# Graph attention over 32 graphs on one core: another opening, from the weights' peaks to the first batch's heads

## What is computed

```python
h = jnp.maximum(_layernorm(x), 0.0)
q, k, v = heads(h @ Wq + bq), heads(h @ Wk + bk), heads(h @ Wv + bv)   # 6 heads of 64
scores = einsum('bhqd,bhkd->bhqk', q, k) / sqrt(64)
probs = softmax(scores + where(adj, 0.0, -9e15), axis=-1)
ctx = einsum('bhqk,bhkd->bhqd', probs, v).reshape(b, s, 384)
out = x + ctx @ Wf + bf
```

## Time and profile before

| | us |
|---|---|
| median of 3 runs | 677.98 |
| lowest and highest | 676.17, 678.21 |
| the profiled execution | 679.02 |
| its span, first to last instruction | 677.0 |

### The profile page before, as it was taken

How to read it: one execution, slowest core, us unless ns; L and a number is a source line. 1 busy time by engine, 2 the same in 40 slices (tenths; PEclk the granted TensorE clock), 3 DMA queues, 4 the chain that set the end, 5 groups by cost and what they waited for, 6 DMA issues and landing times. The chain is left out here.

```text
span 677.0 us, 20551 instructions
## 1 busy us (share of the span) xinstructions
PE 628.2 (93%) x6644; PEld 510.3 (75%) x6644; DVE 513.2 (76%) x1548; ACT 506.7 (75%) x1164; POOL 423.5 (63%) x459
## 2 busy tenths in 40 slices
PE   7638899999899998999999999999999999999985
PEld 5426788888788886888778877788878888888863
DVE  5626787788788877788778887788878888887774
ACT  1435888888788886788878876788778888888872
POOL 1335666767666666776666667576666776676551
PEclk8878899999999999999999999999999999999999
DMA  7015678767787686667877676776878668767563
GB/s 241 20 34 112 127 149 159 154 149 127 160 154 160 150 162 121 150 145 158 159 145 159 153 146 120 154 160 152 159 141 155 146 141 160 160 137 134 127 136 94
DMA packets 207684, 95.89 MB, mean 142 GB/s; under 512 B 152817, under 2 KB 207602, under 8 KB 207602
## 3 DMA queue, kind: packets, MB, share of 16 engines
q1 hardware_dynamic: 207602, 94.69, 67.7%
HBM read 17.05 MB, written 12.58 MB: 44 GB/s over the span
## 5 line engine op out<-in xcount | busy, mean ns | idle before, releaser
L632 DVE CUSTOM_DVE_ANT_0 logits<-scores,mask,logit_unscale 128x256 f32<-128x256 f32 x384 | 170.6, 481 | 128.0 <-PE scores L916 124.6
L432 POOL TENSOR_TENSOR p_rows<-probs,p_rows 128x512 f16<-128x512 f32 x128 | 151.0, 1180 | 183.1 <-ACT p_rows L513 183.1
L503 ACT ACTIVATE probs<-logits,raised 128x256 f32<-128x256 f32 x384 | 174.2, 500 | 6.3
L856 PE MATMUL ring<-h_hi,w_hi 128*128 128x256 f16 x576 | 159.1, 276 | 2.6 <-DVE w_lo L723 2.6
L857 PE MATMUL ring<-h_lo,w_hi 128*128 128x256 f16 x576 | 158.8, 276 | 0.0
L858 PE MATMUL ring<-h_hi,w_lo 128*128 128x256 f16 x576 | 158.6, 275 | 0.0
L416 POOL TENSOR_TENSOR split<-qk,split 128x512 f16<-128x512 f32 x96 | 111.1, 1157 | 13.1 <-DVE split L656 13.1
L915 PE MATMUL scores<-heads 128*128 128x256 f16 x384 | 95.3, 275 | 23.0 <-DMA heads<-split 16.9
L499 ACT ACTIVATE raised<-least,p_raise 128x2 f32<-128x2 f32 x192 | 56.8, 296 | 68.4 <-DVE least L632 53.3
L525 ACT ACTIVATE qk<-ring,qk_bias_s,qkv_ratio 128x256 f32<-128x256 f32 x192 | 97.0, 555 | 9.4 <-PE ring L858 8.6
L943 PE MATMUL ctx<-v_hi,p_cols 128*128 128x65 f16 x768 | 89.5, 194 | 14.0 <-DMA p_cols<-p_rows 9.8
(11 more groups left out here) (90 smaller groups left out, 1427.2 us busy)
## 6 DMA issues: line engine op xcount, KB each, us to landing
heads<-split SPq DMA_DIRECT2D x192, 96.0 KB, 2.2
x_in<-in_x_dram SPq DMA_DIRECT2D x32, 384.0 KB, 3.4
heads<-split SPq DMA_DIRECT2D x192, 64.0 KB, 2.1
out_dram<-result SPq DMA_DIRECT2D x64, 192.0 KB, 2.1
adj_in<-in_adj_dram SPq DMA_DIRECT2D x32, 64.0 KB, 2.0
p_cols<-p_rows SPq DMA_TRANSPOSE x128, 3.1
w_raw<-in_L_gnn_Wq_dram SPq DMA_DIRECT2D x1, 576.0 KB, 4.3
w_raw<-in_L_gnn_Wk_dram SPq DMA_DIRECT2D x1, 576.0 KB, 6.3
```

The costliest lines, as they stand in the source:

```text
L432: pool.tensor_tensor(p_rows[u][:, 1], probs[u % 3][:], p_rows[u][:, 0], ALU.subtract).then_inc(p_lo_ready, 1)
L503: act.activation(probs[u % 3][:, a], logits[u % 3][:, a], ACT.Exp, bias=raised[u % 3][:, a:a + 1], scale=-1.0).then_inc(probs_ready, 1)
L632: dve.tensor_tensor_reduce(out=logits[u % 3][:, a], in0=score_bank[u % 2][:, a * S:(a + 1) * S], in1=mask[b.parity][:, t], scale=logit_uns ...
L856: pe.matmul(out_ap, a_hi, m_hi, start=first, stop=False)
```

## The change

- The joining over partitions no longer uses `partition_all_reduce`. TensorE transposes the peak column, broadcast to 128 columns, into a bank (`spread_peaks`), and VectorE reduces it over its free axis (`join_peaks`).
- There are three joins instead of two: q's and k's peaks with their biases, then v's, then Wf's. Each is followed by `powers` for its own columns, so v's scale no longer comes with those of q and k.
- The factors (`qkv_ratio` for q and k, `logit_unscale`, `mask_scale`, `qk_bias_s`) are made on GpSimd by eight small operations, that of v on VectorE.
- The biases are loaded from ScalarE's queue, at its very start; ScalarE then runs one `Exp` ahead of everything.
- The cycle with b.k = -1 is gone. Its work is written out in the preambles of the engines in another order, with 14 more warm-up matmuls on TensorE between the spread of the peaks and the first projection.
- Batch 0's v is projected and split in cycle 0, behind the second unit; Wv's peak, scale and parts come behind those of q and k. Wf's peak, scale and parts move to other places of cycle 0.
- `bf_full` is copied by ScalarE instead of VectorE.
- SyncE issues `place_heads(0, 0)`, `place_heads(0, 1)` and the load of the third adjacency ahead of cycle 0.
- `project_qk(b, 1)` waits for `v_lo` of the batch before, where it had no such wait (batches 1 and 2).

```diff
+WARM_UPS_MORE = 14
...
-            for k in range(-1, FIRST_IN_LOOP):
+            for k in range(FIRST_IN_LOOP):
...
-            def load_column(dst, src):
-                sp.dma_start(dst, src.rearrange("(c p) -> p c", p=P),
-                             allow_slow_non_contiguous=True).then_inc(small_in, 16)
-            load_column(qk_bias[:, 0], bq)
-            load_column(qk_bias[:, 1], bk)
-            load_column(bv_col[:], bv)
-            sp.dma_start(bf_row[:], bf.rearrange("(a n) -> a n", a=1)).then_inc(small_in, 16)
+            place_heads(Batch(0, 0), 0)
+            place_heads(Batch(0, 0), 1)
+            sp.wait_ge(mask_ready, 2)
+            load_adj(Batch(0, 2))
...
-            pool.wait_ge(peak_ready, 6)
-            pool.partition_all_reduce(qkv_peak_all[:], qkv_peak[:], P, ALL_MAX).then_inc(peaks_joined, 1)
-            pool.wait_ge(factors_ready, 2)
+            def chained(count):
+                pool.wait_ge(pool_chain, count)
+            pool.wait_ge(small_in, 64)
+            pool.wait_ge(scales_ready, 1)
+            pool.tensor_tensor(qkv_ratio[:, 0:2], qkv_scale[:, 2:4], qkv_unscale[:, 0:2],
+                               ALU.mult).then_inc(pool_chain, 1)
+            pool.tensor_tensor(logit_product[:, 0:1], qkv_unscale[:, 2:3], qkv_unscale[:, 3:4],
+                               ALU.mult).then_inc(pool_chain, 1)
+            pool.tensor_tensor(logit_product[:, 1:2], qkv_scale[:, 2:3], qkv_scale[:, 3:4],
+                               ALU.mult).then_inc(pool_chain, 1)
+            for n in range(2):
+                pool.tensor_scalar(qk_bias_s[:, n], qk_bias[:, n], qkv_scale[:, 2 + n:3 + n], None,
+                                   ALU.mult).then_inc(factors_ready, 1)
+            chained(3)
+            pool.tensor_scalar(qkv_ratio[:, 0:2], qkv_ratio[:, 0:2], 1.0 / H_SCALE, None,
+                               ALU.mult).then_inc(factors_ready, 1)
+            pool.tensor_scalar(logit_unscale[:], logit_product[:, 0:1], -1.0 / D ** 0.5, None,
+                               ALU.mult).then_inc(factors_ready, 1)
+            pool.tensor_scalar(mask_scale[:], logit_product[:, 1:2], -NEG * D ** 0.5, None,
+                               ALU.mult).then_inc(factors_ready, 1)
+            pool.wait_ge(factors_ready, 5)
+            make_mask(Batch(0, 0))
+            split_lo(Batch(0, 0), 0)
+            normalise(Batch(0, 1))
+            split_lo(Batch(0, 0), 1)
+            split_lo(Batch(0, 0), 2)
+            pool.wait_ge(bf_ready, 1)
+            add_bias(Batch(0, 0))
...
-                    if first:
-                        pool.wait_ge(peak_ready, 7)
-                        pool.partition_all_reduce(f_peak_all[:], f_peak[:], P, ALL_MAX).then_inc(peaks_joined, 1)
-                        pool.wait_ge(bf_ready, 1)
...
+            def load_column(dst, src):
+                act.dma_start(dst, src.rearrange("(c p) -> p c", p=P),
+                              allow_slow_non_contiguous=True).then_inc(small_in, 16)
+            load_column(qk_bias[:, 0], bq)
+            load_column(qk_bias[:, 1], bk)
+            load_column(bv_col[:], bv)
+            act.dma_start(bf_row[:], bf.rearrange("(a n) -> a n", a=1)).then_inc(small_in, 16)
+            act.wait_ge(pool_const, 5)
+            act.activation(bv_wide[:, 0], zeros[:], ACT.Exp).then_inc(table_loaded, 1)
+            act.wait_ge(table_loaded, 1)
+            h_hi_part(Batch(0, 0))
+            act.wait_ge(scales_ready, 1)
+            for j in range(C):
+                for n in range(2):
+                    weights_hi(n, pair(j))
+            act.wait_ge(factors_ready, 5)
+            qk_full(Batch(0, 0), 0)
             act.wait_ge(small_in, 64)
...
             for c in range(C):
                 act.activation(bv_wide[:, c], zeros[:], ACT.Identity,
                                bias=bv_col[:, c:c + 1]).then_inc(wide_ready, 1)
+            qk_full(Batch(0, 0), 1)
+            qk_full(Batch(0, 0), 2)
+            act.wait_ge(bias_ps_ready, 1)
+            act.activation(bf_full[:], ctx_bank[:, 0:H], ACT.Copy).then_inc(bf_ready, 1)
+            act.wait_ge(scales_ready, 2)
+            weights_hi(2)
-                if front and not first:
+                if front:
+                    if b.k != 0:
+                        v_hi_part(b, 1)
+                    exps(b, 1)
+                if b.k == 0:
+                    v_hi_part(b, 0)
-                    exps(b, 1)
+                if here:
...
-                if b.k == 0:
-                    act.wait_ge(scales_ready, 2)
-                    weights_hi(3)
+                if b.k == 0:
+                    act.wait_ge(scales_ready, 3)
+                    weights_hi(3)
...
+            def join_peaks(spread, cols, nth):
+                dve.wait_ge(peaks_spread, nth)
+                n = cols.stop - cols.start
+                dve.tensor_reduce(peak_all[:, cols], spread[:, 0:n * P].rearrange("p (n q) -> p n q", n=n), AX_X,
+                                  ALU.max).then_inc(peaks_joined, 1)
+                dve.wait_ge(peaks_joined, nth)
...
+            join_peaks(pt_bank, slice(0, 4), 1)
...
+            powers(slice(0, 4), qkv_bound, qkv_scale, qkv_unscale, 1)
             h_lo_part(Batch(0, 0))
-            dve.wait_ge(peaks_joined, 1)
...
-            weights_lo(0, 1, pair(0))
-            weights_lo(1, 2, pair(0))
...
-            dve.wait_ge(factors_ready, 2)
+            for j in range(C):
+                for n in range(2):
+                    weights_lo(n, 2 * j + n + 1, pair(j))
+            qk_hi_part(Batch(0, 0), 0)
+            layer_stats(Batch(0, 1), (0, 1))
+            qk_hi_part(Batch(0, 0), 1)
+            weight_peak(2, peak[:, 4:5])
+            qk_hi_part(Batch(0, 0), 2)
+            join_peaks(pt_bank, slice(4, 5), 2)
+            step(dve.tensor_scalar(qkv_bound[:, 4:5], peak_all[:, 4:5], LEAST, None, ALU.max),
+                 dve.tensor_scalar(qkv_bound[:, 5:6], peak_all[:, 4:5], float(H), LEAST, ALU.mult, ALU.max))
+            powers(slice(4, 6), qkv_bound, qkv_scale, qkv_unscale, 2)
+            step(dve.scalar_tensor_tensor(out=qkv_ratio[:, 2:3], in0=qkv_scale[:, 5:6], scalar=1.0 / H_SCALE,
+                                          in1=qkv_unscale[:, 4:5], op0=ALU.mult, op1=ALU.mult))
+            weights_lo(2, 7)
-                dve.wait_ge(peaks_joined, 2)
+                join_peaks(ring[1], slice(5, 6), 3)
...
-                if front and not first:
+                if front:
-                if first:
-                    weights_lo(0, 3, pair(1))
-                    weights_lo(1, 4, pair(1))
-                    weights_lo(2, 5)
+                if b.k == 0:
+                    v_lo_part(b, 0)
+                if here:
                     v_lo_part(b, 1)
                 if (b + -2).exists():
                     finish(b + -2, 1)
-                if first:
-                    weights_lo(0, 6, pair(2))
-                    weights_lo(1, 7, pair(2))
-                    dve.wait_ge(bias_ps_ready, 1)
-                    dve.tensor_copy(bf_full[:], ctx_bank[:, 0:H]).then_inc(bf_ready, 1)
                 if b.k == 0:
-                    scale_output()
+                    weight_peak(3, peak[:, 5:6])
+                    layer_stats(b + 2, (0, 1))
...
-                if first:
-                    layer_stats(b + 2, (0, 1))
...
-                if first:
+                if b.k == 0:
+                    scale_output()
-                if b.k == 0:
-                    weights_lo(3, 8, pair(0))
-                    weights_lo(3, 8, pair(1))
...
-                    weights_lo(3, 8, pair(2))
+                    weights_lo(3, 8)
...
+                elif j == 1 and (b + -1).exists():
+                    wait(pe, v_lo_ready, (b + -1).count(2, 1))
-                        pe.wait_ge(w_lo_ready, 2 * j + n + (2 if j == C - 1 else 1))
+                        pe.wait_ge(w_lo_ready, 2 * j + n + 1)
...
-                    pe.wait_ge(w_lo_ready, 5)
+                    pe.wait_ge(w_lo_ready, 7)
...
+            def spread_peaks(bank, cols):
+                for n in range(cols.start, cols.stop):
+                    o = (n - cols.start) * P
+                    mm = pe.transpose(bank[:, o:o + P], peak[:, n:n + 1].to_broadcast([P, P]), ident[:])
+                mm.then_inc(peaks_spread, 1)
+            pe.wait_ge(peak_ready, 4)
+            spread_peaks(pt_bank, slice(0, 4))
+            for _ in range(WARM_UPS_MORE):
+                pe.matmul(ring[2][:, 0:P], zeros[:], zeros[:], start=True, stop=True)
+            for j in range(C):
+                project_qk(Batch(0, 0), j)
...
+            pe.wait_ge(peak_ready, 5)
+            pe.wait_ge(peaks_joined, 1)
+            spread_peaks(pt_bank, slice(4, 5))
...
-                if front and not first:
+                if front:
+                if b.k == 0:
+                    project_v(b, 0)
+                    project_v(b, 1)
...
+                if b.k == 0:
```

(42 more changed lines are left out.)

34 lines of the change are left out of this document (8 added, 26 removed).

## The result

| | before | after |
|---|---|---|
| time, median (range) of 4 runs each | 678.10 (676.17 to 680.93) us | 685.32 (685.06 to 686.99) us |
| span of the profiled execution | 677.0 us | 683.4 us |
| first `apply_probs(0, 3)`, the mark | 70.08 us | 55.48 us |
| batch that holds a jump back of the loop, mean of five | 20.96 us | 24.54 us |

The ratio is 1.0097, with a 95% interval from 1.0068 to 1.0126: slower by 1%, where 660.7 us was forecast. The opening did what was forecast (14.6 us earlier at the mark, 15.8 forecast); the loop, which nobody edited, gave it all back and 7 us more.

A forecast was written before the change was run, and what follows sets the result against it. TensorE's work was taken to bound the loop, a chain of waits the opening. An earlier mark (15.8 us) plus saved half clock (1.5) gave 17.3 off 679.02, 661.7; less 1.04 to the median, 660.7 us, range 655.8 to 667.0.

The forecast's parts named there:

- What bounds the kernel: Loop bound by TensorE's work (busy 98.7 us of 100), opening by a chain of waits; nothing in the loop edited.
- Loads: Opening: biases moved to ScalarE's queue cost Wk between 0 and 2.0 us, taken as 1.2.
- Joins: Opening, joining the peaks: four transposes 0.65 us, one reduction 0.6 to 0.7, done at 12.1, scale at 13.3.
- Weights and projections: Opening: weight parts start at 13.3 us, first projection at 14.9 at full clock, projections end at 20.8.
- Factors: Opening: eight tiny operations on GpSimd, 0 to 6 us in all, taken as 1.5 and hidden by the weights.
- Batch 0: Opening: scores of units 0 and 1 at 23.9 and 28.1 us, `split_lo(1, 0)` at 44.2 against 56.05.
- The mark: First `apply_probs(0, 3)` at 54.3 us against 70.08, gain 15.8; with 1.5 of half clock saved, 17.3.
- The sum: Whole run: 679.02 us less 17.3 is 661.7; less 1.04 from profiled execution to median, 660.7.
- (a) to (c): Three rivals; the middle one: GpSimd stays the bound, gain 11.9 us, 666.1; chance 0.17, dear factors included.
- (a): Rival, opening: no clock falls on TensorE and biases come free; gain 20.3 us, time 657.7; chance 0.21.
- (c): Rival, opening: GpSimd's standstills are not due to `partition_all_reduce`, 13.9 us come back; gain 3.4, 674.6; chance 0.04.
- (d): Rival, loop: TensorE waits each cycle on GpSimd's chain, clock falls, 1.5 us each; slower, up to 705.7; chance 0.02.

The follow-up runs named there:

- e3: The kernel after with its hardware loop written out, so no jump back: 657.64 us, ratio 0.9668 to before.
- e4: The kernel before with its hardware loop written out, so no jump back: 673.72 us, ratio 0.9900 to before.
- e1: The kernel after with 44 empty TensorE instructions ahead of its first cycle, moving the loop's head: 654.51 us, ratio 0.9621 to before.
- e5: The kernel before with 112 empty TensorE instructions in cycle 0, loop head at 1482 as in e1: 670.02 us, ratio 0.9854 to before.
- e8: The kernel before, loop written out as in e4, with only Wf's peak joined by TensorE and VectorE instead of GpSimd: 663.62 us, ratio 0.9745.
- e14: The kernel after with 145 empty TensorE instructions ahead of its cycles; single execution, only the loop read: 21.15 us for a batch with a jump.
- e13: The kernel after with 256 empty TensorE instructions ahead of its cycles; single execution, only the loop read: 24.27 us for a batch with a jump.
- e12: The kernel after with 44 empty instructions where TensorE waits, and v's join, scale and split moved behind unit 0: 652.35 us, ratio 0.9585.

## Why the prediction was wrong, step by step

- *What bounds the kernel.* Right for the opening. Wrong in one sentence, "Nothing in the loop is edited", from which I took "the loop's period unchanged": the sum has no term for the jumps back. The 1.3 us of idle in the earlier trace rows were read as a rounding of a full TensorE. 0.91 of them were the standstill of one jump (340.48), and the word "issue" beside `scores` at 184.21, 261.59 and so on stood in the trace of before. I had read that word as a cause on GpSimd and never asked for it on TensorE.
- *Loads.* 1.2 taken; Wk is 0.58 later (8.05 to 8.63), nearer to the lower end.
- *Joins.* Four transpositions 0.65 as forecast, the reduction 0.69 (0.6 to 0.7), done at 11.54 (12.1).
- *Weights and projections.* `w_hi` at 12.67 (13.3), first projection at 14.36 (14.9) at full clock, as forecast.
- *Factors.* 1.5 taken, 2.55 measured: eight operations of 0.19 to 0.56 us. They end at 15.34, and `qk_full` began at 16.59: hidden.
- *Batch 0.* Scores of units 0 and 1 at 23.54 and 27.48 (23.9, 28.1). `mask_and_max(0, 0)` at 28.49 (27.8): of v's tiny steps, three took 0.51, 0.92 and 0.71 beside GpSimd's `split_lo` and `add_bias`, where the first two had taken 0.17 in the first join. The larger miss is the clock. I gave TensorE half clock for some 3.5 us behind its gap; it had it from 29.2 to 36.0, 6.8 us. So the 18 matmuls of v, taken as 2.9 us at full clock, ran from 31.31 to 36.56, 5.2 us, and `v_lo(0, 1)` ended at 38.0 (35.4). `layer_stats(2)` then ends at 40.8 (38.3), `split_lo(1, 0)` at 46.5 (44.2). Ahead of `apply_probs(0, 1)` I gave half clock once more; that did not come, the clock is 1.00 from 36 to 70.

```profile
30.00:35.00 5.00, 4.60 (x16) 2.57 (x17) 1.13 (x5) 2.52 (x6) 0.00 (x0) 0.50 0.30 86
...
36.00:70.00 34.00, 27.69 (x287) 22.29 (x286) 25.83 (x80) 25.09 (x57) 23.25 (x25) 1.00 0.51 102
```

- *The mark.* 55.48 (54.3). With no jumps the opening is worth 16.1 us (e3, e4); with jumps that cost nothing 15.8 (e1, e5), or about 13.8 without the empty instructions; against 17.3. So this term was 1.2 to 3.5 too large. The mark itself is 1.2 late, with `layer_stats(2)` 2.5 late ahead of it; what each part of the delay costs at the mark no run took apart.
- *The sum* left out a term, and this is the step that made a gain into a loss: five jumps at 24.54 - 20.96 = 3.6 us, 17.9. With it and the tail (34.5 us behind the last `add_bias`, 33.0 before) the spans come out: 677.0 - 13.6 + 18.5 + 1.5 = 683.4.
- *The rivals.* (a) to (c) did not happen; (a)'s full clock is refuted by the half clock from 29.2 to 36.0, (c) by e8. (d) had the mechanism, a repeated wait of TensorE with a fall of the clock, and came at 0.02 because I put it on GpSimd's chain and gave "the loop's code is untouched" as the reason against it. The code was untouched; its place was not. The price that I gave, 1.5 us a time from 12 times on, was of no use either: it was 3.6, at five places.

## What to carry to other kernels

An edit ahead of a hardware loop moves the loop in the instruction stream, and that alone changed this kernel by up to 31 us of 685. Count the instructions of the bounding engine ahead of and in the loop, look at its waits for "issue" at each jump back and at the packets of the instruction queue; and before a part of a change is judged by its time, place the loop's head alike in both (e1 and e5), or write the loop out (e3 and e4). GpSimd's second `partition_all_reduce`, 0.4 us by itself, held the engine for 13.9 us in all, and taking it out was worth 10.5 us (e8); transpositions with one reduction on VectorE take its place, 1.4 us for four columns (10.16 to 11.54).

## What the runs showed of the hardware that I had not expected

- A jump back of a loop of 1738 TensorE instructions makes its batch 0, some 2.1 to 2.3, or 5.4 to 6.2 us longer, by the head's place in its block of 256, and 21 or 65 packets go with it. Where between 72 and 109 the edge lies, and why 18 instructions over seven blocks do no harm, is open.
- An instruction that only increments a semaphore costs TensorE some 0.15 us, not the 0.1 that my expectations used. Ahead of the first scores of batch 0, 44, 145 and 256 of them (e1, e14, e13) left standstills of 4.46, 19.97 and 37.07 us; both steps give 0.154 each, with some 2.3 us of the whole hidden behind earlier work:

```profile
27.98 0.37 PE L951 MATMUL scores<-heads 128*128 128x256 f16 x1 [4.46 <-issue]
```

```profile
43.92 0.37 PE L951 MATMUL scores<-heads 128*128 128x256 f16 x1 [19.97 <-issue]
```

```profile
60.53 0.37 PE L951 MATMUL scores<-heads 128*128 128x256 f16 x1 [37.07 <-issue]
```

- Some of VectorE's smallest operations, 0.17 us alone, took up to 0.92 us while GpSimd ran a `tensor_tensor`, and where the end of such an operation is shown, the slow one ended with it (24.62 against 24.59, 26.51 against 26.49). In e12, where GpSimd had just become idle, the last three of v's steps took 0.17, 0.17 and 0.16. Others, the reciprocal of 0.17 at 25.60 in the kernel after, were not slowed beside GpSimd; what sets them apart is open.
- Keeping the clock up by idle matmuls is worth 1.5 us here, and by where it pushed the loop the same 14 matmuls cost 18.
